# Two gated cross-attention layers with experts on one core: scatters and gathers issued in a row behind the scores, keys spread before two of the exponentials, first-layer values of two batches per product

## The reference, cut to what matters

```python
x = x + tanh(g_xattn[0]) * attention0(layernorm(x), ctx, ctx)
x = x + tanh(g_ffn[0])   * experts0(layernorm(x))     # 8 experts, the best 2 per token
x = x + tanh(g_xattn[1]) * attention1(ctx, ctx, layernorm(x), mask)
x = x + tanh(g_ffn[1])   * experts1(layernorm(x))     # 4 experts, all computed, weighed

def attention0(Q, K, V):                              # per batch, 64 queries by 64 keys
    q, k, v = Q @ Wq + bq, K @ Wk + bk, V @ Wv + bv
    p = softmax(q_h @ k_h.T / sqrt(8))                # for each of 16 heads h
    return concat_h(p @ v_h) @ Wo + bo
```

## Time and profile before

| | us |
|---|---|
| median of 3 runs | 1203.03 |
| lowest, highest | 1202.12, 1204.2 |
| the profiled execution | 1202.05 |
| its span | 1200.3 |
| TensorE busy | 1083.8 (90%) |
| VectorE busy | 894.5 (75%) |
| ScalarE busy | 794.5 (66%) |
| GpSimd busy | 543.2 (45%) |
| first-layer scores, first and last | 14.01, 345.79 |
| first expert row product | 405.46 |
| second-layer scores, first and last | 678.46, 966.06 |

### The profile page before, as it was taken

How to read it: one execution, slowest core, us unless ns; L and a number is a source line. 1 busy time by engine, 2 the same in 40 slices (tenths; PEclk the granted TensorE clock), 3 DMA queues, 4 the chain that set the end, 5 groups by cost and what they waited for, 6 DMA issues and landing times.

```text
span 1200.3 us, 38909 instructions
## 1 busy us (share of the span) xinstructions
PE 1083.8 (90%) x13205; PEld 918.0 (76%) x13205; DVE 894.5 (75%) x3003; ACT 794.5 (66%) x1739; POOL 543.2 (45%) x699
## 2 busy tenths in 40 slices
PE   7799999997885499999999699999999988999998
PEld 4677777775763499999999567666666767999997
DVE  5678887886777445545545779899898878988886
ACT  4788888886671255555555489999998964444443
POOL 2114555556547344344343676676666431222230
PEclk7999999999897699999999899999999999999999
DMA  7223211111101233333332211111221100000000
GB/s 195 86 86 94 78 55 54 53 51 56 49 22 55 82 98 102 96 93 96 93 95 77 57 50 49 50 48 47 51 50 46 32 2 10 27 17 17 26 17 27
DMA packets 116776, 71.81 MB, mean 60 GB/s; under 512 B 51736, under 2 KB 105240, under 8 KB 116632
## 3 DMA queue, kind: packets, MB, share of 16 engines
q1 hardware_dynamic: 108440, 53.13, 16.2%
q0 software_dynamic: 8192, 16.79, 4.5%
HBM read 45.88 MB, written 22.94 MB: 57 GB/s over the span
## 4 chain that ended last, share of the span: by engine, by line
PE 69%; DVE 10%; ACT 7%; issue 7%; SPq 4%; another core or an unknown queue 1%; POOL 1%; DMA 1%; DVEq 0%; ACTq 0%; POOLq 0%
PE ps_m L1902 11%; PE ps_p L1656 6%; PE ps_p L1781 5%; PE ps_m L1781 4%; PE ps_s L1613 4%; PE ps_p L1671 4%; PE ps_s L1888 3%; PE ps_s L1889 3%; PE ps_s L1890 3%; PE ps_s L1623 3%; PE ps_m L1639 3%; PE ps_s L1769 2%; PE ps_s L1771 2%; PE ps_s L1770 2%; PE ps_m L1588 2%
## 5 line engine op out<-in xcount | busy, mean ns | idle before, releaser
L776 ACT ACTIVATE PT<-ps_p 128x512 f32<-128x512 f32 x320 | 184.4, 596 | 32.3 <-PE ps_p L1656 18.2
L1080 DVE TENSOR_REDUCE mx<-ps_s 128x8 f32<-128x512 f32 x256 | 169.3, 683 | 36.8 <-PE ps_s L1613 23.4
L877 ACT ACTIVATE Kbd<-ps_s,c 128x512 f32<-128x512 f32 x128 | 87.4, 687 | 113.9 <-PE ps_s L1771 113.6
L592 POOL TENSOR_TENSOR spare<-spare 1x1 f32<-1x1 f32 x99 | 21.4, 216 | 295.0 <-DVE b1s L1459 152.1
L675 POOL DMA_INDIRECT w1a<-louts,gi x128 | 125.2, 978 | 54.9 <-issue 31.2
L1656 PE MATMUL ps_p<-cst,Pr 128*128 128x128 f32 x1024 | 148.6, 279 | 0.6 <-DVE orow L1376 0.4
L1902 PE MATMUL ps_m<-xn3T 128*128 128x128 f32 x1136 | 137.9, 275 | 0.0
L1902 PEld LDWEIGHTS ps_m<-xn3T 128*128 128x128 f32 x1136 | 132.7, 192 | 0.0
L958 ACT ACTIVATE xn3T<-ps_s,b1s 128x256 f32<-128x256 f32 x284 | 111.7, 474 | 28.3 <-PE ps_s L1890 28.3
L1656 PEld LDWEIGHTS ps_p<-cst,Pr 128*128 128x128 f32 x1024 | 121.6, 145 | 2.4 <-issue 1.7
L632 POOL DMA_INDIRECT lists<-xn3T,pos x80 | 78.4, 980 | 81.1 <-DVE mx L1080 54.2
(11 more groups left out here) (229 smaller groups left out, 2818.8 us busy)
## 6 DMA issues: line engine op xcount, KB each, us to landing
xn3T<-lists SPq DMA_DIRECT2D x71, 128.0 KB, 2.1
louts<-xn3T SPq DMA_DIRECT2D x71, 128.0 KB, 1.8
ctxg<-in_ctxT SPq DMA_DIRECT2D x32, 256.0 KB
Kbd<-in_ctxT SPq DMA_DIRECT2D x512, 8.0 KB
out<-x SPq DMA_DIRECT2D x16, 256.0 KB, 2.3
w1a<-in_L_ffn_W SPq DMA_DIRECT2D x8, 256.0 KB
w2a<-in_L_ffn_W SPq DMA_DIRECT2D x8, 256.0 KB
Pr<-in_ctxT SPq DMA_DIRECT2D x16, 128.0 KB, 2.3
```

The costliest lines, as they stand in the source:

```text
L776: return nc.scalar.activation(dst, src, ACT.Copy)
L1080: V.tensor_reduce(mx[g.par][:, q, :], per_key(ps_s[:, q, :]), AX, ALU.max).then_inc(max_done, 1)
```

## The change

**Values.** The context is loaded once per batch instead of twice (`ctxg` becomes 2 planes of 4x64, of which the first layer uses one). A product takes two batches, 2 calls a group instead of 4. Each half of the partitions now holds another batch, so four copies of 128 columns spread them: ScalarE does the odd batches (2 copies, after the heads' copy instead of before it), VectorE the even batches (`values_even`, 2 copies from PSUM, new, ahead of `denominators`). The PV product waits for both.

**Keys.** The keys' and queries' product moves to `bank6` and ahead of the PV product; it waits for the residual sum (`x1_ready`), which VectorE now does before the maximum of bank 0. ScalarE spreads the keys before the exponentials of banks 0 and 1, two spreads on either side of `sums_out`. TensorE's projection moves ahead of the tokens' transpose.

**Indirect DMAs.** The first four scatters of a step are issued one after another once all scores of the step are done (`s_done`), the others after the inverse deviations. The second layer's first three gathers go in a row behind the scores too, the fourth after the inverse deviations. Scatters are due one step later (`LAG = 9`), `LAST_ROWS` is redrawn, and `route_places` of the regular blocks moves from the start of a step to its last third.

**Handover.** `warm(40)` also waits for the scatters of group 29.

```diff
+LAG = 9
-LAST_ROWS = {24: ((16, 0, 1), (17, 0)), 25: ((17, 1), (18, 0, 1)), 26: ((19, 0, 1), (20, 0)), 27: ((20, 1), (21, 0, 1)),
+LAST_ROWS = {25: ((16, 0, 1), (17, 0)), 26: ((17, 1), (18, 0, 1)), 27: ((19, 0, 1), (20, 0)), 28: ((20, 1), (21, 0, 1)),
...
-        ctxg = [sb(f"ctxg{i}", [P, 4, 2, S]) for i in range(2)]
+        ctxg = [sb(f"ctxg{i}", [P, 2, 4, S]) for i in range(2)]
...
+        def spread_from(batch, head):
+            rows = bank7[S * batch:S * batch + S, 0:GT]
+            return rows.rearrange("p (b j i d) -> p b j i d", b=2, j=8, i=2)[:, :, :, head, :]
+
+        def spread_to(g, batch, head):
+            rows = Vbd[g.par][S * head:S * head + S, :, :, DK * head:DK * head + DK]
+            return rows.rearrange("p (b n) j d -> p b n j d", n=2)[:, :, batch, :, :]
...
-        kq_bank, lg_bank, rk_bank = (ps_s[:, i, :] for i in range(3))
+        kq_banks = (bank6, ps_s[:, 0, :])
...
                 if g.layer == 0 and g.k >= GROUPS:
+                    early = {GROUPS: 3, GROUPS + 1: 5}.get(g.k, 0)
+                    for row in rows_due(g.k)[:early]:
+                        scatter(*row)
                     if have(-2):
                         inverse_deviations(g)
-                    if g.k == GROUPS:
-                        pool.wait_ge(pv_done, g.plus(-1).count(4, 4))
-                    for row in rows_due(g.k):
+                    for row in rows_due(g.k)[early:]:
                         scatter(*row)
...
                 if have(0):
-                    pool.wait_ge(max_done, g.count(4, 1))
+                    pool.wait_ge(s_done, g.count(4, 4))
                 if g.layer == 0:
-                    scatter_at(g, "A")
+                    for row in rows_due(g.k)[:4]:
+                        scatter(*row)
                 elif have(4):
                     gather(g.plus(4), 0, 0)
+                    gather(g.plus(4), 0, 1)
+                    gather(g.plus(4), 1, 0)
...
                 if have(-2) or have(2):
                     inverse_deviations(g)
-                if g.layer == 1 and have(4):
-                    gather(g.plus(4), 1, 0)
+                if g.layer == 0:
+                    for row in rows_due(g.k)[4:]:
+                        scatter(*row)
+                elif have(4):
+                    gather(g.plus(4), 1, 1)
                 if have(-1) and not (g.layer == 0 and g.k > LATE_SUMS):
                     rows_plus_constant(g.plus(-1))
...
+            def values_even(g):
+
+                wait(dve, pv_done, g.count(4, -4))
+                dve.wait_ge(v_done, g.count(1, 1))
+                V.tensor_copy(spread_to(g, 0, 1), spread_from(0, 1))
+                V.tensor_copy(spread_to(g, 0, 0), spread_from(0, 0)).then_inc(v_even, 1)
...
-                for b in range(4):
-                    ins = mm(bank7[:, P * b:P * b + P], ctxg[g.par][:, b, :, :].rearrange("p i k -> p (i k)"), wv[0][:, :],
-                             start=True, stop=True)
+                for b in range(2):
+                    ins = mm(bank7[:, P * b:P * b + P], ctxg[g.par][:, 0, 2 * b:2 * b + 2, :].rearrange("p b k -> p (b k)"),
+                             wv[0][:, :], start=True, stop=True)
...
             pe.wait_ge(pos_ready, BLOCKS)
+            pe.wait_ge(scattered[(GROUPS - 3) % STEPS], 64 * GROUPS // STEPS)
             warm(40)
```

More of the change, by code:

```diff
@@ L1264, in step @@
                         layer1_constants()
[L1265 to L1267 removed]
+                    placed = router_due(g, -5, 1)
+                    if placed and not placed.in_main():
+                        route_places(placed, placed.k not in AT_ONCE)
                     now(maximum, 0, 2)
@@ L1300, in step @@
                         first_choice(g.plus(-3))
+                    if placed and placed.in_main():
+                        route_places(placed, True)
+                    now(values_even, 1)
                     now(denominators, -1)
@@ L1798, in step @@
                     now(probs_turned, -1, 1)
+                    if g.k < GROUPS:
+                        now(project_out, -2)
                     now(tokens_turned, 1)
```

95 lines of the change are left out of this document (43 added, 52 removed).

## The result

The changed kernel takes 1231.29 us (median of 4, 1230.47 to 1233.4) against 1202.57 before: a ratio of 1.0229, 95% interval 1.0199 to 1.0259. It is slower, where 1174.5, a range of 1162 to 1194 and "faster" were forecast. The profiled execution has a span of 1229.4 us, 29.1 more than before.

| stage | before | after | difference | forecast |
|---|---|---|---|---|
| first scores to step 4 of the first layer | 44.25 | 41.96 | -2.3 | -1 |
| steps 4 to 24 | 201.57 | 213.92 | +12.4 | -6.3 |
| steps 24 to 31 | 85.96 | 81.07 | -4.9 | -11.5 |
| step 31 to the second layer's first scores | 332.67 | 329.01 | -3.7 | -2.5 |
| second layer, 31 steps | 287.60 | 319.04 | +31.4 | -7 |

A forecast was written before the change was run, and what follows sets the result against it. TensorE bounds regular first-layer steps, VectorE block steps; indirect DMAs hold TensorE's signals elsewhere. Savings 6.3 + 11.5 + 2.5 + 1 + 7 = 28.3 off 1202.05, plus 0.98 for the median: 1174.5 us, range 1162 to 1194.

The forecast's parts named there:

- Second layer: Second layer: fifteen holds of 0.75 us go, three gathers in a row are past before the PV product; 7 us saved.
- PV product: First layer, steps 24 to 31: the row's fourth scatter still crosses the PV product; 0, up to 0.46 us a step free.
- The slower rival: Steps with a row: it holds the heads' transpose signal, +1.5 us a step in both layers; 1250 us, chance 0.06.
- Regular steps at 9.0: First layer's regular steps: 9.83 less 0.54 for values and 0.29 for keys gives 9.0 us.
- the values' passes: TensorE in first-layer steps: four passes instead of eight take 0.54 us from the engine that bounds the step.
- Block steps at 11.9: First layer, every fourth step, set by VectorE: from 10.95 to 11.9 us, by two new copies and a later entry.
- the 0.35 behind it: Block steps: VectorE enters about 0.35 us further behind TensorE, as the step before is shorter for TensorE only.
- the rival "rounds gain nothing": First layer's four-step rounds: block steps at 12.5 or more, so no gain, some holds remain; 1186 us, chance 0.19.
- Steps 24 to 31: First layer's end: six holds of 2.3 to 2.4 us go, five before step 31; 74.5 against 85.96, 11.5 us saved.
- the 1181 of the prediction: Total if VectorE's SBUF work slows scatters: rows end some 0.6 us later, sum about 7 us higher; left out.
- five rounds of 1.34: First layer, steps 4 to 24: five four-step rounds, each 39.15 against 40.49 us; 6.3 us saved (0 to 18).
- the best case: Whole kernel: PV products free of the row, second layer gives its full 11.4; 39.4 us saved, 1162, chance 0.15.

The follow-up runs named there:

- the one-place experiment: Changed kernel with one or a few second-layer gathers per step at one place after another, others left out; steps 8.57, 8.57, 9.3, 9.16, 8.95, 9.97 us.
- the doubled matmuls: Changed kernel with scatters and gathers in four new slots, and the values' two matmuls issued twice; 1172.5 us, ratio 1.0166 to the kernel before.

## Why the prediction was wrong

- **The mechanism was named, and its place and reach were read wrongly.** The prediction's sum put the rows where "the signals of the scores are out" and took it that a burst means scores and PV product. Second transposes and the queries' product are one too, and a hold lasts to the end of the whole row and up to 0.9 us more. The step that failed first is *Second layer*: "Three gathers in a row at 1.4 to 5.0 us are past before the PV product". The third ended 5.04 us in, as forecast, but the product began at 4.94 and stopped until 5.89, and the second copy of the transposes, which no term of the sum names, came 1.84 late; for -7 us came +31.
- **PV product**: "crossed as before, gain and loss 0". It was crossed by the end of a row instead of a single scatter: 2.27 us instead of 1.55. With the queries' copy that it held (1.44 late) this is the 1.5 us a step that turned -6.3 into +12.4.
- **The slower rival** had 6 in 100 and the right price, "+1.5 us" a step, for the wrong signal: the heads' copy was prompt in every step with a row (1.52 to 1.70 us into it), 1.84 us were lost at a later signal of the second layer (1.0 in two of the experiments). That a case at "+1.5 us" came nearest is luck in the number, not in the signal. Both rows held against it were from places with no burst behind the DMA: a single gather, which the one-place experiment shows to be free behind the scores, and the drain. They say nothing of a row.
- **Regular steps at 9.0**: right, 8.92 where no DMA is in them. But of the 0.7 taken from 9.62, the values' passes are 0.17 by the doubled matmuls, since something else, perhaps ScalarE, comes next; the rest is left for the keys' order, which no run tried alone.
- **Block steps at 11.9**: 12.62 came. VectorE's 0.6 was right (12.55 to 11.94 without it), the 0.35 behind it too small. On the chips without holds the round of four gains 0.69 three times and gives back 1.3 in the block step, and where the clock falls 1.2 more: the rival "rounds gain nothing" was right there.
- **Steps 24 to 31** gained 4.9 of 11.5: the old holds went, but the row across the products came here too, and on the chip without holds the change costs 3.6 in this stretch. The parts without a row of DMAs across a product came out better than forecast: start 2.3 for 1, drain and handover 3.7 for 2.5.
- **The holds' cost was taken for the kernel's.** It is that of one chip: elsewhere the kernel before has none, and the change has another reason to be slower, POOL's addition beside VectorE's operations, a move that the prediction passed over (only the gathers' new place was priced, not what stands behind the last of them on POOL). The 1.55 of a crossed PV product and the holds of the earlier trace rows, from which the prediction argued, are that chip's too. The rows' scatters last 0.96 to 1.03 us as before, so longer rows (the 1181 of the prediction) are not the reason.
- **Two sums are off** without changing anything: five rounds of 1.34 are 6.7, not 6.3, and the best case is 1202.05 - 39.4 + 0.98 = 1163.6, not 1162.

What stays open: what in a chip makes an indirect DMA's issue hold TensorE's signals (the DMA lasts the same 0.96 to 1.03 with holds and without), and why the same row of three held the copy for 1.84 in one kernel and 1.0 in two others where the kernel before takes 1202.8.

## What to carry to other kernels

When a transfer is moved off one burst of signals, list every burst that it now crosses, and count the whole row with what it holds back at its end; a shorter step moves everything behind it. Price also the instruction that a moved DMA pushes along on its own engine, and on which engine's operation that falls. A cost seen as waits on nothing that the profile shows ("issue", "remote") may belong to the chip: look at the same kernel on another one before building on it.

## What the runs showed of the hardware

- The same kernel takes 1202.8 us on one chip and 1153.3 to 1153.6 on three others. 35 of the 45 us between two profiles lie in the two stretches where the first shows waits on TensorE's signals beside indirect DMAs; the 7.9 of the handover were not traced further.
- On the chip with holds, one gather across the PV product costs 0.73 us, two in a row across the second transposes 0.4, three 1.4; across nothing, 0. On the second chip rows of two and three at these places left the step at 8.56, and on the third a scatter across the PV product left that product at 1.09.
- VectorE's operations of 0.15 and 0.28 us took 0.64 to 0.69 and 0.92 to 0.94 beside POOL's gather and addition, on chips with and without holds.
- Behind three of five block steps, at whose end TensorE had waited 1.1 us for `rank`, its clock fell to 1.2 GHz, and the next step was 1.2 us longer (10.13 for 8.93); with four idle matmuls in the wait it fell behind none of the five, and the block steps were 0.27 longer.
